# Attention scores on one core: one signal of two for each pair of score products, in place of one signal each

## What is computed

```python
attn = jnp.einsum('bhqd,bhkd->bhqk', query, key) / scale
attn = jax.nn.softmax(attn, axis=-1)
out = jnp.einsum('bhqk,bhkd->bhqd', attn, value)
```

## Time and profile before

| | us |
|---|---|
| median of 3 runs | 3142.26 (3140.79 to 3144.47) |
| the profiled execution, its own time | 3138.19 |
| its span, first to last instruction | 3136.1 |
| mean granted TensorE clock | 0.983 |
| attention, first to last score product | 672.5 to 2303.7 |

### The profile page before, as it was taken

The page is one execution under the profiler, slowest core; times in us unless marked ns, Lnnn a source line. Parts: engine busy times, 40 slices in busy tenths (PEclk is TensorE's granted clock), DMA queues, the critical chain, the costliest instruction groups (busy, mean ns, idle before and its releaser), DMA issues. The chain is left out here.

```text
span 3136.1 us, 42811 instructions
## 1 busy us (share of the span) xinstructions
PE 3022.8 (96%) x15468; PEld 2016.3 (64%) x15468; DVE 2239.5 (71%) x3351; ACT 1487.5 (47%) x2714; POOL 2093.0 (67%) x715
## 2 busy tenths in 40 slices
PE   7999999989999999999999999999967999999998
PEld 4888888855555555555555555555525777877776
DVE  4555556568777777777777777777628778678784
ACT  1222222226666666666666666666742223223232
POOL 0211112118999999999999999999944665666663
PEclk8999999989999999999999999999988999999999
DMA  3554545664656464655656464646243323313311
GB/s 105 173 183 167 177 168 177 188 152 107 137 115 145 99 146 107 139 119 126 132 123 140 108 145 98 149 109 135 52 125 87 108 62 99 107 54 107 107 54 41
DMA packets 188922, 381.78 MB, mean 122 GB/s; under 512 B 17088, under 2 KB 53088, under 8 KB 180704
## 3 DMA queue, kind: packets, MB, share of 16 engines
q1 hardware_dynamic: 179696, 313.70, 36.3%
q0 software_dynamic: 9072, 66.06, 10.3%
HBM read 194.59 MB, written 118.49 MB: 100 GB/s over the span
## 5 line engine op out<-in xcount | busy, mean ns | idle before, releaser
L278 DVE TENSOR_REDUCE part_max<-ps_m 128x1 f32<-128x512 f32 x1984 | 1213.8, 681 | 333.9 <-PE ps_m L262 333.0
L950 POOL TENSOR_TENSOR pairs<-probs 128x2048 f32<-128x2048 f32 x255 | 1179.8, 4632 | 144.6 <-ACT probs L923 131.8
L923 ACT ACTIVATE probs<-ps_s 128x512 f32<-128x512 f32 x2048 | 1036.6, 623 | 292.7 <-PE ps_s L815 276.8
L262 PE MATMUL ps_m<-k_stack,q_stack 96*128 96x512 f32 x1984 | 820.3, 415 | 15.0 <-DVE neg_max L275 8.2
L815 PE MATMUL ps_s<-q_stack,k_stack 97*128 97x512 f32 x2048 | 817.1, 402 | 5.6 <-PEq L311 3.6
L262 PEld LDWEIGHTS ps_m<-k_stack,q_stack 96*128 96x128 f32 x1984 | 376.7, 190 | 287.7 <-DVE part_max L278 136.7
L828 PE MATMUL ps_o<-probs,v_tiles 128*32 128x512 f32 x4096 | 495.6, 602 | 0.0
L815 PEld LDWEIGHTS ps_s<-q_stack,k_stack 97*128 97x128 f32 x2048 | 388.0, 190 | 130.0 <-ACT probs L923 21.2
L541 POOL TENSOR_TENSOR ln_rstd<-ln_rstd,ln_minus_half 128x4 f32<-128x4 f32 x16 | 16.1, 1009 | 415.9 <-DVE ln_rstd L584 415.9
L957 POOL TENSOR_TENSOR pairs<-pairs 128x2048 f32<-128x2048 f32 x63 | 288.4, 4578 | 4.9
L828 PEld LDWEIGHTS ps_o<-probs,v_tiles 128*32 128x32 f32 x4096 | 107.3, 109 | 234.5 <-issue 176.6
(11 more groups left out here) (180 smaller groups left out, 4809.8 us busy)
## 6 DMA issues: line engine op xcount, KB each, us to landing
pairs<-pairs POOLq DMA_DIRECT2D x63, 1024.0 KB, 8.5
q_stack<-q_hi_scratch SPq DMA_DIRECT2D x128, 256.0 KB, 6.2
k_stack<-k_hi_scratch SPq DMA_DIRECT2D x64, 512.0 KB, 10.7
x_in<-in_x SPq DMA_DIRECT2D x16, 1024.0 KB, 5.4
q_hi_scratch<-st_hi SPq DMA_DIRECT2D x64, 256.0 KB, 2.2
q_lo_scratch<-st_lo SPq DMA_DIRECT2D x64, 256.0 KB, 2.5
k_hi_scratch<-st_hi SPq DMA_DIRECT2D x64, 256.0 KB, 2.4
k_lo_scratch<-st_lo SPq DMA_DIRECT2D x64, 256.0 KB, 2.6
```

What stands on the lines that cost most here:

```text
L262: nc.tensor.matmul(bank[:, :], att["q"][r][0:ROWS, half, h, q * P:(q + 1) * P], att["k"][r][0:ROWS, h, kc * CH:(kc + 1) * CH], start=True, ...
L278: nc.vector.reduce_max(part_max[:, half, j, kc:kc + 1], bank[:, :], AX).then_inc(att["m_read"], 1)
L923: nc.scalar.activation(probs[:, (r * UNITS + u) % PR, x // HG, x % HG, :], ps_s[place(u * UT + x) % SR][:, :], ACT.Exp, scale=SCALE).then_ ...
L950: nc.gpsimd.tensor_tensor(pairs[:, w, :, :], probs[:, (r * UNITS + u) % PR, 0, :, :], probs[:, (r * UNITS + u) % PR, 1, :, :], ALU.add).th ...
```

## The change

A score product signals `scored` only when its place x in the unit is odd, and then by two. ScalarE waits only ahead of the even Exps, for the count that includes the odd score behind. Both engines issue the same products and Exps in the same order; `exped`, the three banks and all other waits are as before.

```diff
                 if v >= SR or not is_first(n):
                     pe.wait_ge(exped, taken(n, v - SR))
-                nc.tensor.matmul(ps_s[v % SR][:, :], ks[r][:, a, kt * P:(kt + 1) * P],
-                                 qs[r][:, qc, a, :], start=True, stop=True).then_inc(scored, 1)
+                m = nc.tensor.matmul(ps_s[v % SR][:, :], ks[r][:, a, kt * P:(kt + 1) * P],
+                                     qs[r][:, qc, a, :], start=True, stop=True)
+                if x % 2 == 1:
+                    m.then_inc(scored, 2)
...
                     for x in range(UT):
-                        act.wait_ge(scored, n * TILES + u * UT + x + 1)
+                        if x % 2 == 0:
+                            act.wait_ge(scored, n * TILES + u * UT + x + 2)
                         nc.scalar.activation(probs[:, (r * UNITS + u) % PR, x // HG, x % HG, :], ps_s[place(u * UT + x) % SR][:, :],
                                              ACT.Exp, scale=SCALE).then_inc(exped, 1)
```

## The result

The changed kernel takes 3392.61 us (median of 4 runs, 3391.3 to 3392.85) against 3143.36 us (4 runs, 3140.79 to 3147.57): a ratio of 1.079 (95% interval 1.078 to 1.081), 7.9% slower. The profiled execution took 3392.75 us. The forecast was 3386 us, range 3300 to 3430.

What follows compares the result with a forecast made beforehand. TensorE was taken to set the pace, with GpSimd some 3 us per group behind. 235.2 (groups 1 to 30) + 6.6 (group 31) + 1.5 (group 0) = 243.3 us more gave 3386 us, range 3300 to 3430.

Steps and rivals of the forecast that it cites:

- (a): Each even Exp waits for the odd score behind it: exp 0 starts at 1.33 us of the unit, not 0.86.
- (b): Odd scores and even Exps close a loop: 1.27 us per turn against 0.94 of TensorE's work, units 1.02 us longer.
- (g): 1024 fewer TensorE signals and ScalarE waits: taken as nothing, bounds 0 and a gain of 10 us.
- (c): The one unit per group with the transposed maximum starts the loop only after neg_max: 0.70 us longer.
- (d): Groups 1 to 30 together: 7.84 us longer per group, 235.2 us in all.
- (e): Group 31, without maximum products and paced by ScalarE: eight units 0.83 us longer each, 6.6 us.
- the clock rival: TensorE's idle time in each turn lowers its granted clock: 3429 us, or 3470 and more; chance 0.12.
- (f): Group 0: first two units' lengthening hidden behind a load from memory, units 2 to 7 together 1.5 us longer.
- (h): GpSimd's additions and the queues' DMAs do not move the time; no transfer is on the path in groups 1 to 30.
- a waited-for product does lose its preload: Rival claimed the opposite: weights already in when the wait ends, a turn of 1.17 us, 3307 us; chance 0.09.
- GpSimd would hide a part: Rival: GpSimd as pace-maker hides up to 3 us per group, 4.8 us left of 7.84, 3294 us; chance 0.03.
- a gain from fewer signals would decide: Rival: halving TensorE's signals shortens units and the loop is absent: 3132 or about 3115 us; chance of faster 0.03.

Runs made afterwards that it cites:

- wait_only: The changed kernel's paired wait on ScalarE, but every score product signals by one as in the kernel before: 3342.3 us, ratio to before 1.063.
- not_31: The change in groups 0 to 30 only, with the single signals of the kernel before in group 31: 3379.0 us, ratio to before 1.075.
- last_pair: The kernel before with only scores 6 and 7 of each unit paired, the others signalled and waited for singly: 3145.1 us, ratio to before 1.001.
- pair_by_one: The changed kernel with its one signal per pair adding one instead of two, ScalarE counting pairs: 3341.4 us, ratio to before 1.063.
- two_each: The kernel before with every score product signalling by two and ScalarE waiting for each one singly: 3145.7 us, ratio to before 1.001.

## Why the prediction was right, point by point

- *TensorE sets the pace and no score of it waits for ScalarE*: right. What the loop put on TensorE's sequence went onto the time: the middle groups' starts hold 234 of the 254.6 us.
- *(a)* Exp 0 at 1.33 of the unit: 1.33.
- *(b)* One turn 1.27, unit 6.82: 1.25 and 6.83. The loop is right, but that its size came out so closely is luck: two errors cancel. From an Exp to the weight load I took 0.65, and it is 0.71, because I did not see that the wait of a product which adds two stands in an instruction ahead of the weight load; (g) priced the change of signals at 0, with 10 us of gain as its bound, and in fact it costs 50. From the weight load to the next Exp I took 0.62, and it is 0.54. I had read that at S0 and exp 0 of group 31, and exp 0 is the one Exp of a unit behind further waits (`pv_done`, `pair_done`): in the trace a semaphore instruction of ScalarE stands 0.08 ahead of it. The other Exps follow their score without it, as wait_only's rows show. Up to PV a unit has three of the first step and two of the second: 0.18 too little and 0.16 too much. The shorter second step could be read before the change, in the unit of the earlier trace rows, where exp 3 waits for S3 in mid-unit and starts 0.43 behind its start, 0.04 behind its end:

```profile
1524.62 0.40 PE L815 MATMUL ps_s<-q_stack,k_stack 97*128 97x512 f32 x1
...
1525.05 2.56 ACT L923 ACTIVATE probs<-ps_s 128x512 f32<-128x512 f32 x5 [0.40 <-PE ps_s L815]
```

With that step, and the rest of the sum as it stood, the turn is 1.19 and the forecast about 3347 us: close to wait_only's 3342, and 45 too low for the change.
- *(c)* 0.70 for the unit with the transposed maximum: 7.09 in place of about 6.46 from first score to first score, 0.63, by the same shorter turn.
- *(d)* 7.84 per group, 235.2 us: 7.80 and 234.0. The group of 51.0 us that the prediction names is the attention's length over 32, with group 0 (65.5 us) in it; a middle group took 50.64, so 58.8 should have read 58.5.
- *(e)* 6.6 us in group 31: 15.3. The units that kept the clock took 6.34, as 5.51 + 0.83 said; four others took 8.5 or, with sums, some 11. The rest is the clock rival's, which the prediction left outside its sum, at 1.4 us for a fall. It held in group 31 alone: the middle group of the row for 1700 to 1751 us stayed at 1.00. About 5 of the 15.3 us come of the base, as not_31's 51.8 us for a group 31 with single signals show.
- *(f)* 1.5 us in group 0: -0.8. Units 0 and 1 are hidden behind the load, as said. From the product behind that load to the first score of group 1 it is 47.2 us in place of 47.3, so units 2 to 7 show nothing of the 1.5.
- *(h)* GpSimd and the transfers: right. GpSimd waits 212.3 us for ScalarE in place of 62.3.
- Not in the sum: 3.8 us ahead of the attention and 2.4 behind it, where the kernels are the same. Over the profiles of all these kernels the first score starts between 672.5 and 676.3 us, at 672.5 in last_pair and at 675.6 in wait_only; what moves it was not looked for.
- *The sum*: 243.3 us for the two profiled executions, where 254.6 were measured. The forecast is only 6.6 us off because the medians lie 249.3 apart, and not 254.6.

The rivals: a waited-for product does lose its preload (0.50 in wait_only, in place of 0.40). That GpSimd would hide a part, and that a gain from fewer signals would decide, have fallen: with 1024 signals fewer, pair_by_one takes the same 57.0 us per middle group as wait_only. By the Trainium skill, "TensorE: Matmul & The Clock Gate", section "The cost: per-tile semaphore tail", 1024 increments at 26.3 ns each would have given at most 27 us, an estimate. These products, of 97 rows and 128 columns each and 0.234 us apart, don't show it. That the signal by two would not work has fallen by the run itself.

**Still open.** What exactly makes the clock fall in some units of group 31 and not in others: before had one fall there, two_each and last_pair took 50.7 us against 46.9 with hardly another program in that group, not_31 took 51.8 us with the program of before in it, and with the change in group 31 alone the group took 63.8 us against 62.1 in the whole change. Also open are the few us ahead of the attention.

## What to carry to other kernels

Joining two signals into one means that the consumer starts on the first tile when the second is done. Where producer and consumer share a ring of few banks, look for the loop that this closes: with a ring of three and pairs of two, only one tile is left to run ahead. Add up one turn (consumer, its signal, weight load, product, its signal) and hold it against the producer's own work over the pair: 1.19 to 1.25 us against 0.94 here, 0.25 to 0.3 us for each turn. A bank more opened the loop here, and the same edit cost nothing in the middle groups. Pairing only the last two tiles before a break cost nothing that could be told either. And 1024 signals fewer were worth nothing, though TensorE, which gave them, sets the pace.

## What the runs showed of the hardware

- In all these runs a product that adds two to a semaphore has its wait in an instruction of its own ahead of the weight load. Its load starts 0.71 us after the start of the Exp that it waits for, against 0.65 for a product that adds one, whose load carries the wait. Where the wait is already satisfied, 1983 more instructions cost 2.0 us by the medians, not told from nothing. L857 had shown that such a product works, not that it is free.
- The same on ScalarE: exp 0, whose wait for its score stands in an instruction of its own, starts 0.11 to 0.12 us after the score's end, an Exp that carries that wait itself 0.04.
- In the changed kernel TensorE's clock fell from 2.4 to 1.2 GHz (0.50 from 2505 to 2510 us) in group 31, where TensorE had two scores per 1.25 us and a block of value products between. In the middle groups, with four products per 1.25 us, it was 1.00. With 56 added products that nobody reads, group 31 too was at 1.00 and 6.8 us shorter.
